# First FFN of a macaron block on one core: norm factors and gates by ScalarE's logarithm and exponential instead of GpSimd's power

## The chip, the cores and the metric

One core of one Trainium2 chip. The metric is device time in microseconds of one execution; several executions are timed and the median is given. The profile is of one execution more, with its own time.

## The reference, cut to what matters

Input x is 8 batch rows of 1024 tokens of 256 numbers, all float32. Three parts follow each other:

```python
x = x + 0.5 * ffn(layernorm(x), ...)
x = x + attn(layernorm(x), ...)
x = x + 0.5 * ffn(layernorm(x), ...)
...
# ffn: 8 experts of 128 hidden units, the best two of each token are used
logits = x @ router_w + router_b
top, idx = top_k(softmax(logits), 2)
top = top / sum(top)                       # the two gates
h = gelu(einsum('btd,nde->btne', x, W1) + b1)
out = sum((einsum('btne,nef->btnf', h, W2) + b2) * mask_with_gates, experts)
# layernorm: (x - mean) / sqrt(var + 1e-5)
```

With l1 and l2 the largest and second largest logit of a token and e = exp(l2 - l1), the two gates are 1/(1+e) and e/(1+e). The kernel puts the factor 0.5 into them, so it computes g1 = 1/(2(1+e)) and g2 = e*g1.

## The kernel before, in words

The core runs five instruction streams (TensorE is PE, VectorE DVE, ScalarE ACT, GpSimd POOL, SyncE SP). Each is written out in program order and meets the others by semaphores.

**First FFN.** Only the two experts that a token chose are computed. The routing runs row by row. A row is 1024 tokens, held as 8 tiles of 128 tokens in one of four buffers `xb` (row r in buffer r % 4). For a row: load (`row_load`, SP); mean and variance (`row_stats`, L1399, DVE, in two halves); the norm's factors rs = (var + eps)^-0.5 and nm = -mean * rs (`row_rstd`, L1899, POOL, with the ALU's power); x * rs + nm in place (`row_norm`, L1123, ACT, in two halves); turn by 128x128 transposes (`row_turn`, L809, PE, copied out by ACT, `row_turned`); logits (`row_logits`, L819, and back to tokens on partitions by `row_logits_turn`, L829); ranks of the logits, the choice and l2 - l1 (`row_route`, L1415, DVE); e = euler ^ (l2 - l1) (`row_exp`, L1913, POOL, power again); both gates into `share` (`row_gates`, L1445, DVE); counting by matmuls of the chosen pattern (`row_spots`, L836, PE) and from it the place of each token in each chosen expert's region (`row_spots`, L1455, DVE). Then `send` (L1917, POOL) issues 16 indirect DMAs per row, one for each tile and choice, which scatter the normed tokens (1 KB each, 128 KB a DMA) to DRAM regions `spots_d`, sorted by expert.

Rows are taken in three batches, rows 0-1, 2-4 and 5-7. When a batch's last row has its spots, `batch_table` (L1478, DVE) makes the table of its blocks: 23, 31 and 31, together 85 **steps** of 256 tokens of one expert. SP then fills each region's end with zeros (`pads`, L587, 8 DMAs of 256 KB) and waits for all sends of the batch (`block_load`, L594). A step is: load a block of 256 tokens (SP); turn it (`block_turn`, PE, L853); copy out (`block_x`, ACT, L1149) with a copy of the expert's W1 (`w1_copy`, ACT, L1164); first matmuls (`block_hidden`, PE, L862); GELU (`block_gelu`, ACT, L1170); second matmuls (`block_out`, PE, L877); add the bias and copy out (`block_left`, DVE, L1538); store to `made_d` (SP).

**What sets the order.** All of it is laid out on hand-written **ticks**. Each engine runs `for tau in range(TICKS)` and in tick tau issues its part of step tau - STEP0 (turn and copy at +0, hidden at +1, GELU at +2, out at +3, bias at +4, store at +5, load at -3) and of every row r whose start `ROW_AT[r]` plus a fixed offset is tau:

| offset | work of a row |
|---|---|
| -5 | load (rows 4 to 7) |
| 0, 1 | statistics, DVE |
| 2 | norm factors, POOL |
| 3, 4 | norm, ACT |
| 4, 5 | turn, PE and ACT |
| 6, 7 | logits, PE and ACT |
| 8 | routing, DVE |
| 9 | count, PE; e, POOL |
| 10 | spots, gates and, at a batch's end, the table, DVE |
| 11 to 16 | sends, three a tick, POOL |
| 12 | at a batch's end, the homes, DVE |

A tick has no clock of its own: an engine goes on as soon as its semaphores allow. Within a tick the order is that of the loop's body (L1039 PE, L1319 ACT, L1773 DVE, L2015 POOL, L635 SP). On SP a tick issues the block store, then the block load, then the row load. The split of the attention's weights in a high and a low part (`split`, six pieces) goes on ACT on the ticks 14, 16 to 24 and on DVE on the ticks 15, 17 to 25.

**After it.** From tick `ROW0` on the first row's results are fetched by indirect DMA (`fetch`, L1925) and added to x with the factors `share` (`combine`, L1541). Then follow 320 attention items over `slots()` and the second FFN, dense over all experts, in 16 groups. The attention's first projections are copied out only after the last step's hidden matmuls (`evac`, L1241), and VectorE goes on only when the last blocks are stored (L1812).

The instruction on which the change turns, L1908:

```python
pool.tensor_tensor(rs_a[:, :], vt_a[:, :], half_a[:, :], ALU.pow).then_inc(s_ars)
```

## Time and profile before

| | us |
|---|---|
| median of 3 executions | 2147.09 (2142.99 to 2148.42) |
| profiled execution, its own time | 2143.95 |
| its span, first to last instruction | 2142.2 |
| TensorE busy | 1899.1 (89%) |
| VectorE busy | 1389.8 (65%) |
| ScalarE busy | 1175.3 (55%) |
| GpSimd busy | 1126.9 (53%) |

The span and the busy times are of the profiled execution. In the rows below an engine's name is followed by the line of the kernel and the operation; `q` behind a name is that engine's queue (register, semaphore and DMA-issuing instructions); "<-" names what ended an idle time, and "remote" or "another core or an unknown queue" is a release that the profile can't place. A busy time doesn't count what the engine waited.

### The profile page before, as it was taken

Reading aid. Unit: us, or ns where it says so; the run is one execution under the profiler, and the core shown is the slowest. Engines: PE = TensorE matmul, PEld = TensorE weight load, DVE = VectorE, ACT = ScalarE, POOL = GpSimd, SP = SyncE. Lnnn points to the kernel's source line nnn. Section 1 sums busy time; section 2 is a strip of 40 time slices with the busy share of each in tenths; the row PEclk is TensorE's granted clock in tenths of the full one; section 3 lists DMA queues with packets and bytes.
Section 4 is the critical chain, followed back from the end, with each engine's and each line's share of the span. In section 5 each row is a group of like instructions: output and inputs, shape, how many; then the busy total and the mean of one; then the engine's idle time right before and its main releaser. Section 6 shows DMA issues by size and latency. Waiting matters only on the chain.

```text
span 2142.2 us, 37969 instructions
## 1 busy us (share of the span) xinstructions
PE 1899.1 (89%) x11764; PEld 1409.7 (66%) x11764; DVE 1389.8 (65%) x4781; ACT 1175.3 (55%) x2936; POOL 1126.9 (53%) x1253
## 2 busy tenths in 40 slices
PE   4377877968998998998998998998999999999998
PEld 2155566845665666665665665665676688888887
DVE  5343344476586585685685685685664488888887
ACT  4244444645557556556556556656555555555554
POOL 5745434157277277377376386386354444444444
PEclk8678988989999999999999999999999999999999
DMA  8557576611031031031031031030023111111110
GB/s 291 194 170 260 197 255 231 233 57 33 1 94 40 1 97 38 1 97 38 1 102 33 1 104 31 3 105 28 1 58 116 37 33 38 40 41 39 36 36 30
DMA packets 106575, 173.64 MB, mean 81 GB/s; under 512 B 13296, under 2 KB 64904, under 8 KB 105480
## 3 DMA queue, kind: packets, MB, share of 16 engines
q1 hardware_dynamic: 83336, 118.42, 16.7%
q0 software_dynamic: 20736, 52.52, 7.8%
q8 instruction: 97, 1.59, 0.3%
q14 instruction: 102, 0.84, 0.1%
q10 hardware_dynamic: 2304, 0.28, 0.1%
HBM read 80.33 MB, written 90.84 MB: 80 GB/s over the span
## 4 chain that ended last, share of the span: by engine, by line
PE 46%; DVE 16%; issue 13%; POOL 12%; ACT 8%; DMA 2%; another core or an unknown queue 1%; SPq 1%; DVEq 0%; ACTq 0%; POOLq 0%
PE bank L720 6%; PE bank L722 5%; PE bank L721 5%; PE bank L1009 4%; PE bank L998 4%; PE bank L969 4%; PE bank L980 4%; PE bank L940 3%; POOL spots_d L1923 3%; ACT prob L1292 2%; POOL prob L1970 2%; DVE x L1550 2%; DVE st L1381 2%; PE bank L971 1%; PE bank L877 1%
## 5 line engine op out<-in xcount | busy, mean ns | idle before, releaser
L1970 POOL TENSOR_TENSOR prob<-prob,rden 128x512 f32<-128x512 f32 x320 | 337.2, 1055 | 452.7 <-DVE rden L1756 449.1
L1292 ACT ACTIVATE prob<-prob,nmax 128x256 f32<-128x256 f32 x512 | 256.0, 502 | 401.8 <-DVE nmax L1738 393.4
L1738 DVE CUSTOM_DVE_ANT_0 prob<-bank,mask 128x256 f32<-128x256 f32 x512 | 195.4, 418 | 105.0 <-PE bank L969 103.5
L1625 DVE SCALAR_TENSOR_TENSOR xb<-bank,gate,xb 128x256 f32<-128x256 f32 x512 | 211.9, 477 | 55.6 <-PE bank L722 55.1
L969 PE MATMUL bank<-kT,qT 64*128 64x256 f32 x1024 | 213.2, 434 | 22.2 <-DVE nmax L1738 21.6
L1885 POOL TENSOR_TENSOR hl<-hf,hh 128x512 fp32r<-128x512 f32 x128 | 164.6, 1291 | 113.9 <-ACT hh L1109 109.2
L980 PE MATMUL bank<-ident,prob 128*128 128x128 f32 x1280 | 199.3, 279 | 20.7 <-POOL prob L1970 20.7
L980 PEld LDWEIGHTS bank<-ident,prob 128*128 128x128 f32 x1280 | 153.9, 142 | 79.9 <-POOL prob L1970 33.3
L1750 DVE COPY probT<-bank 128x512 f32<-128x512 f32 x160 | 110.2, 688 | 117.5 <-PE bank L980 116.6
L1108 ACT ACTIVATE hf<-bank,b1s 128x512 f32<-128x512 f32 x128 | 88.2, 689 | 171.2 <-PE bank L722 167.7
L998 PE MATMUL bank<-probT,V 128*64 128x128 f32 x2048 | 170.7, 288 | 9.1 <-ACT oT_s L1308 7.7
L1538 DVE TENSOR_TENSOR yout<-bank,b_all 128x512 f32<-128x512 f32 x85 | 58.0, 690 | 174.4 <-remote 71.5
L1957 POOL DMA_INDIRECT hs_d<-yr,place x128 | 129.8, 1014 | 44.5 <-issue 32.8
L969 PEld LDWEIGHTS bank<-kT,qT 64*128 64x128 f32 x1024 | 94.9, 188 | 86.5 <-issue 48.2
L998 PEld LDWEIGHTS bank<-probT,V 128*64 128x64 f32 x2048 | 108.8, 137 | 64.4 <-issue 61.0
L1923 POOL DMA_INDIRECT spots_d<-xb,spot x128 | 125.2, 978 | 48.1 <-issue 36.3
L720 PE MATMUL bank<-w,hh 128*128 128x256 f32 x512 | 146.4, 286 | 3.8 <-POOL hl L1885 2.7
L722 PE MATMUL bank<-w,hh 128*128 128x256 f32 x512 | 144.8, 283 | 0.0
L721 PE MATMUL bank<-w,hl 128*128 128x256 f32 x512 | 144.4, 282 | 0.0
L1009 PE MATMUL bank<-wol,oT_s 128*128 128x256 f32 x512 | 126.3, 390 | 1.2 <-ACT xf_t L1239 1.2
L1770 DVE TENSOR_TENSOR x<-bank,x 128x256 f32<-128x256 f32 x64 | 27.1, 423 | 145.3 <-PE bank L1009 145.3
L877 PE MATMUL bank<-w_st,hf 128*128 x340 | 97.0, 411 | 21.3 <-issue 13.6
(254 smaller groups left out, 5016.7 us busy)
## 6 DMA issues: line engine op xcount, KB each, us to landing
xin<-spots_d SPq DMA_DIRECT2D x85, 256.0 KB
made_d<-yout SPq DMA_DIRECT2D x85, 256.0 KB
x<-in_L_attn_x SPq DMA_DIRECT2D x8, 1024.0 KB
x_d<-x SPq DMA_DIRECT2D x8, 1024.0 KB, 4.4
xb<-x_d SPq DMA_DIRECT2D x16, 512.0 KB, 3.8
out<-xb SPq DMA_DIRECT2D x16, 512.0 KB, 2.9
xb<-in_L_attn_x SPq DMA_DIRECT2D x7, 1024.0 KB
spots_d<-zeros SPq DMA_DIRECT2D x24, 256.0 KB
```

The costliest lines, as they stand in the source:

```text
L720: pe.matmul(o, w[0], x[0], start=start, stop=False)
L721: pe.matmul(o, w[1], x[0], start=False, stop=False)
L722: return pe.matmul(o, w[0], x[1], start=False, stop=stop)
L969: ins = pe.matmul(bank[g % NS][:, 0:KEYS], qT[hs, hp, t * P:(t + 1) * P], kT[hs, hp, t * P:t * P + KEYS], start=True, stop=True)
L980: ins = pe.transpose(bank[3 + j % 2][:, (2 * h + kk) * P:(2 * h + kk + 1) * P], prob[j % NP][:, h, kk * P:(kk + 1) * P], ident[:, :])
L998: ins = pe.matmul(bank[5][h * DH:(h + 1) * DH, hp * P:(hp + 1) * P], V[:, t + kk, hs] if t < T else hv[:, kk, hs], probT[j % 2][:, 2 * h + ...
L1009: ins = pe.matmul(bank[tb][:, 0:D], oT_s[:, ch, :], w[:, ch, :], start=(ch == 0), stop=(ch == HC - 1))
L1292: act.activation(prob[j % NP][:, h, :], src, ACT.Exp, bias=nmax[:, j % 4, h:h + 1], scale=-1.0 if light else 1.0, accum_out=den[:, j % 4, ...
L1625: dve.scalar_tensor_tensor(out=x, in0=bank[ob][:, (t % 2) * D:(t % 2 + 1) * D], scalar=gate[:, k % 2, t, e:e + 1], in1=x, op0=ALU.mult, op ...
L1738: ins = dve.tensor_tensor_reduce(prob[j % NP][:, h, :], bank[g % NS][:, 0:KEYS], mask[:, which, :], -1.0, 3e38, ALU.add, ALU.min, nmax[:, ...
L1923: pool.indirect_dma_start(spots_d[batch_of_row(r)], bass.IndirectOffsetOnAxis(spot[:, r, c, t:t + 1], 0), xb[r % 4][:, t, :], None).then_i ...
L1970: pool.tensor_tensor(prob[j % NP][:, :, :], prob[j % NP][:, :, :], rden[:, j % 4, :].unsqueeze(2).broadcast_to([P, 2, KEYS]), ALU.mult).th ...
```

## The change

Row r's norm factors move from GpSimd to ScalarE and VectorE: `row_rstd` on ScalarE takes ln(var + eps) with the eps as a bias from a new tile `eps_a`, then exp(-0.5 * ln), and VectorE's new `row_shift` makes nm in one instruction. Both are issued at offset 2. The exponential for the gates is taken once, for all eight rows, by ScalarE in tick `SHARES` = 62 (`share_exps`), and VectorE makes all gates in tick 63 (`shares`); `t2nd_a` and `wt_a` grow from 128x8 to 128x64 numbers, and `combine` waits for the new semaphore `s_share`. GpSimd keeps only its set-up, the sends, and what it does for the attention. `STEP0` goes from 26 to 24, the rows 3 to 7 start at 18, 26, 35, 44 and 53 instead of 19, 26, 36, 46 and 56, and the split of the attention's weights runs on every tick from 14 (ACT) and 15 (DVE) on. The tile and semaphore declarations and the set-up of `half_a` and `euler_a`, which `eps_a` replaces, are cut here.

```diff
@@ -314,9 +314,10 @@
             return xb_2[k % 3]
 
 
-        STEP0 = 26
+        STEP0 = 24
         TICKS = STEP0 + STEPS + 6
-        ROW_AT = (0, 6, 12, 19, 26, 36, 46, 56)
+        ROW_AT = (0, 6, 12, 18, 26, 35, 44, 53)
+        SHARES = ROW_AT[-1] + 9
 
         def row_at(tau, after):
 
...
@@ -534,7 +535,7 @@
             return 9 + n if n < 5 else 17 + n
 
         NR = 17
-        NA, NPOS, NTAB = 14, 6, 16
+        NA, NPOS, NTAB = 11, 6, 16
         NHOME = 4
         NRK = 1 + 2 * (4 * T - 2) + 2
         TILES = 10 * ROWS
...
@@ -1119,6 +1120,20 @@
                             ffn_hi(kk, n)
                         elif kind == "gt":
                             ffn_gates(kk)
+
+            def row_rstd(r):
+
+                act.wait_ge(s_amv, 2 * r + 2)
+                act.activation(ln_a[:, :], mv_a[:, :, 1], ACT.Ln, bias=eps_a[:, 0:1]).then_inc(s_aln)
+                act.wait_ge(s_aln, r + 1)
+                if r > 0:
+                    act.wait_ge(s_arstd, r)
+                act.activation(rs_a[:, :], ln_a[:, :], ACT.Exp, scale=-0.5).then_inc(s_ars)
+
+            def share_exps():
+
+                act.wait_ge(s_ra, NA * ROWS)
+                act.activation(t2nd_a[:, :, :], t2nd_a[:, :, :], ACT.Exp).then_inc(s_exa)
 
             def row_norm(r, h):
 
...
@@ -1322,9 +1337,13 @@
                 for s_ in step_at(tau):
                     w1_copy(s_)
                     block_x(s_)
+                for r in row_at(tau, 2):
+                    row_rstd(r)
                 for h in range(2):
                     for r in row_at(tau, 3 + h):
                         row_norm(r, h)
+                if tau == SHARES:
+                    share_exps()
                 for what in tick_jobs(tau):
                     evac(*what)
 
...
@@ -1337,8 +1356,8 @@
                     act.wait_ge(s_small, 16 * 8)
                     for at_ in (0, 32):
                         act.activation(b2_s[at_:at_ + E, :], b2_st[:, :], ACT.Copy).then_inc(s_whi)
-                if 14 <= tau < 14 + 2 * 3 * C and tau % 2 == 0:
-                    i, n = (tau - 14) // 2 % C, (tau - 14) // 2 // C * INNER
+                if 14 <= tau < 14 + 3 * C:
+                    i, n = (tau - 14) % C, (tau - 14) // C * INNER
                     split(wqkv_s[0][:, i, n:n + INNER], wqkv_st[:, i, n:n + INNER], (s_wld[4], 16))
 
                 for q in Y0.get(tau, ()):
...
@@ -1407,7 +1426,7 @@
                 ins.then_inc(s_abn)
                 dve.wait_ge(s_abn, 2 * r + h + 1)
                 if h == 0 and r > 0:
-                    dve.wait_ge(s_avar, 2 * r)
+                    dve.wait_ge(s_aln, r)
                 for q in range(TG * h, TG * h + TG):
                     ins = dve.bn_aggr(mv_a[:, q, :], st_a[:, q, :])
                 ins.then_inc(s_amv)
...
@@ -1438,19 +1457,25 @@
                     dve.wait_ge(s_full, job_no["apos", r - 2, 0] + 1)
                 dve.tensor_scalar(chosen[r % 2][:, 0:T, :], lrank[:, :, :], 2.0, None, ALU.is_lt).then_inc(s_ra)
                 dve.wait_ge(s_ra, n + 8)
-                dve.tensor_reduce(t2nd_a[:, :], l2nd[:, :, :], AX_X, ALU.add).then_inc(s_ra)
+                dve.tensor_reduce(t2nd_a[:, r, :], l2nd[:, :, :], AX_X, ALU.add).then_inc(s_ra)
                 dve.wait_ge(s_ra, n + 10)
-                dve.tensor_tensor(t2nd_a[:, :], t2nd_a[:, :], lmax_a[:, :], ALU.subtract).then_inc(s_ra)
-
-            def row_gates(r):
-                n = NA * r
-                dve.wait_ge(s_exa, r + 1)
-                g = share[:, r, :, :]
-                dve.tensor_scalar(wt_a[:, :], t2nd_a[:, :], 1.0, 2.0, ALU.add, ALU.mult).then_inc(s_ra)
-                dve.wait_ge(s_ra, n + 12)
-                dve.reciprocal(g[:, 0, :], wt_a[:, :]).then_inc(s_ra)
-                dve.wait_ge(s_ra, n + 13)
-                dve.tensor_tensor(g[:, 1, :], t2nd_a[:, :], g[:, 0, :], ALU.mult).then_inc(s_ra)
+                dve.tensor_tensor(t2nd_a[:, r, :], t2nd_a[:, r, :], lmax_a[:, :], ALU.subtract).then_inc(s_ra)
+
+            def row_shift(r):
+
+                dve.wait_ge(s_ars, r + 1)
+                if r > 0:
+                    dve.wait_ge(s_anorm, 4 * r)
+                dve.scalar_tensor_tensor(out=nm_a[:, :], in0=mv_a[:, :, 0], scalar=-1.0, in1=rs_a[:, :], op0=ALU.mult, op1=ALU.mult).then_inc(s_arstd)
+
+            def shares():
+
+                dve.wait_ge(s_exa, 1)
+                dve.tensor_scalar(wt_a[:, :, :], t2nd_a[:, :, :], 1.0, 2.0, ALU.add, ALU.mult).then_inc(s_share)
+                dve.wait_ge(s_share, 1)
+                dve.reciprocal(share[:, :, 0, :], wt_a[:, :, :]).then_inc(s_share)
+                dve.wait_ge(s_share, 2)
+                dve.tensor_tensor(share[:, :, 1, :], t2nd_a[:, :, :], share[:, :, 0, :], ALU.mult).then_inc(s_share)
 
             def row_spots(r):
 
...
@@ -1542,6 +1567,7 @@
 
                 if t == 0:
                     dve.wait_ge(s_ald[b % 2], 16 * (b // 2 + 1))
+                    dve.wait_ge(s_share, 3)
                 x = x1[b % 2][:, t, :]
                 for c, part in ((0, y_row), (1, z_row)):
                     dve.wait_ge(s_got[2 * t + c], 16 * (b + 1))
...
@@ -1776,11 +1802,14 @@
                 for h in range(2):
                     for r in row_at(tau, h):
                         row_stats(r, h)
+                for r in row_at(tau, 2):
+                    row_shift(r)
+                if tau == SHARES + 1:
+                    shares()
                 for r in row_at(tau, 10):
                     row_spots(r)
                     if last_of_batch(r):
                         batch_table(batch_of_row(r))
-                    row_gates(r)
                 for r in row_at(tau, 8):
                     row_route(r)
                 for r in row_at(tau, 12):
...
@@ -1794,8 +1823,8 @@
                 if tau == 13:
                     split(rw_s[:, :, 1, :], rw_st[:, :, :], rw_s[:, :, 0, :], 5)
                     split(b2_s[64:64 + E, :], b2_st[:, :], b2_s[0:E, :], 7)
-                if 15 <= tau < 15 + 2 * 3 * C and tau % 2 == 1:
-                    m = (tau - 15) // 2
+                if 15 <= tau < 15 + 3 * C:
+                    m = tau - 15
                     i, n = m % C, m // C * INNER
                     split(wqkv_s[1][:, i, n:n + INNER], wqkv_st[:, i, n:n + INNER], wqkv_s[0][:, i, n:n + INNER], 8 + m)
 
...
@@ -1896,24 +1925,6 @@
                         rstd(0, k + 1, 2 * k + 2)
                     if s == 9 and k < last:
                         exp2nd(k + 1)
-            def row_rstd(r):
-
-                pool.wait_ge(s_amv, 2 * r + 2)
-                if r > 0:
-                    pool.wait_ge(s_anorm, 4 * r)
-                    pool.wait_ge(s_arstd, r)
-                pool.tensor_scalar(vt_a[:, :], mv_a[:, :, 1], LN_EPS, None, ALU.add).then_inc(s_avar)
-                pool.tensor_scalar(nm_a[:, :], mv_a[:, :, 0], -1.0, None, ALU.mult).then_inc(s_avar)
-                pool.wait_ge(s_avar, 2 * r + 1)
-                pool.tensor_tensor(rs_a[:, :], vt_a[:, :], half_a[:, :], ALU.pow).then_inc(s_ars)
-                pool.wait_ge(s_ars, r + 1)
-                pool.wait_ge(s_avar, 2 * r + 2)
-                pool.tensor_tensor(nm_a[:, :], nm_a[:, :], rs_a[:, :], ALU.mult).then_inc(s_arstd)
-
-            def row_exp(r):
-                pool.wait_ge(s_ra, NA * r + 11)
-                pool.tensor_tensor(t2nd_a[:, :], euler_a[:, :], t2nd_a[:, :], ALU.pow).then_inc(s_exa)
-
             def send(r, i):
 
                 t, c = divmod(i, 2)
...
@@ -2013,10 +2023,6 @@
             pool.memset(mask[WIN:P, 2, 3 * WIN:KEYS], MASKED).then_inc(s_const)
             pool.wait_ge(s_const, CONST)
             for tau in range(TICKS):
-                for r in row_at(tau, 2):
-                    row_rstd(r)
-                for r in row_at(tau, 9):
-                    row_exp(r)
                 for i in range(2 * T):
                     for r in row_at(tau, 11 + i // 3):
                         send(r, i)
```

## Rows read from the trace of the kernel before

**Rows 1.** the page: 40 slices of 53.6 us, TensorE's granted clock and DMA share

```profile
PEclk8678988989999999999999999999999999999999
DMA  8557576611031031031031031030023111111110
```

**Rows 2.** the chain that ended last, 84 to 120 us: start, us, what

```profile
91.73 14.96 another core or an unknown queue
```

**Rows 3.** waits, 86 to 420 us: total, times, longest

```profile
DVE yout L1538 <- remote: 71.5, 8, 13.4
...
ACT xa L1136 <- remote: 28.1, 7, 9.3
```

**Rows 4.** block GELUs (L1170) by sending stretch, then overall: length, busy (x)

```profile
86.90:103.80 16.90, 0.00 (x0) 0.80 0.55 181
111.30:131.30 20.00, 0.93 (x2) 0.82 0.69 231
150.20:176.20 26.00, 1.89 (x4) 0.80 0.80 281
196.10:218.70 22.60, 1.42 (x3) 0.85 0.85 286
242.60:265.10 22.50, 2.33 (x5) 0.92 0.69 232
278.30:298.40 20.10, 1.16 (x4) 0.83 0.71 242
...
86.90:416.50 329.60, 41.86 (x86) 0.87 0.66 223
```

**Rows 5.** the sends, groups by line, 0 to 650 us

```profile
L1923 POOL DMA_INDIRECT spots_d<-xb,spot x128 | 125.2, 978 | 48.1 <-issue 36.3 <-DVE spot L1476 11.8
```

**Rows 6.** timeline of GpSimd: start, us, instruction

```profile
35.07 1.23 POOL L1923 DMA_INDIRECT spots_d<-xb,spot  x1 [0.20 <-issue]
...
75.59 0.25 POOL L1905 TENSOR_SCALAR vt_a<-mv_a 128x8 f32<-128x8 f32 x1
...
78.05 1.64 POOL L1915 TENSOR_TENSOR t2nd_a<-euler_a,t2nd_a 128x8 f32<-128x8 f32 x1
...
102.82 0.96 POOL L1923 DMA_INDIRECT spots_d<-xb,spot  x1 [0.31 <-issue]
...
157.27 0.25 POOL L1905 TENSOR_SCALAR vt_a<-mv_a 128x8 f32<-128x8 f32 x1 [3.53 <-DVE mv_a L1412]
```

**Rows 7.** timeline of SyncE's queue, 40 to 92 us: row load, pads, block reads

```profile
61.29 0.40 SPq L585 DMA_DIRECT2D xb<-in_L_attn_x  x1
62.41 15.65 SPq L592 DMA_DIRECT2D spots_d<-zeros  x8
86.88 5.70 SPq L604 DMA_DIRECT2D xin<-spots_d  x3
```

**Rows 8.** ScalarE: timeline, then table loads by line

```profile
42.14 0.20 ACT L1072 ACTIVATE rw<-rw_st 128x16 fp32r<-128x16 f32 x1
...
106.72 0.60 ACT L1149 ACTIVATE xh<-bank 128x512 f32<-128x512 f32 x1 [14.98 <-remote]
107.33 1.28 ACT L1170 ACT_TABLE_LOAD   x1
108.63 0.47 ACT L1170 ACTIVATE hf<-bank,b1s 128x256 f32<-128x256 f32 x1
...
L1292 ACT ACT_TABLE_LOAD x1 | 1.3, 1283 | 0.0
L1108 ACT ACT_TABLE_LOAD x1 | 1.3, 1283 | 0.0
```

**Rows 9.** DMA issues: count, KB each, us to landing

```profile
xb<-in_L_attn_x SPq DMA_DIRECT2D x2, 512.0 KB, 5.2
```

**Rows 10.** timeline of VectorE at 47.5 us

```profile
47.51 0.17 DVE L1443 TENSOR_TENSOR t2nd_a<-t2nd_a,lmax_a 128x8 f32<-128x8 f32 x1
```

**Rows 11.** every engine between two sending stretches: PE, PEld, DVE, ACT, POOL busy

```profile
218.70:242.60 23.90, 20.83 (x103) 15.42 (x104) 10.15 (x32) 11.81 (x27) 1.68 (x2) 0.86 0.51 162
```

More of the change, by code:

```diff
@@ L181, in build @@
         e_row = sb("e_row", [P, len(BATCH), E])
-        half_a, euler_a = sb("half_a", [P, T]), sb("euler_a", [P, T])
+        eps_a = sb("eps_a", [P, 1])
         st_a, mv_a = sb("st_a", [P, T, 6]), sb("mv_a", [P, T, 2])
-        vt_a, rs_a, nm_a = sb("vt_a", [P, T]), sb("rs_a", [P, T]), sb("nm_a", [P, T])
+        ln_a, rs_a, nm_a = sb("ln_a", [P, T]), sb("rs_a", [P, T]), sb("nm_a", [P, T])
         chosen = [sb(f"chosen{i}", [P, T + 1, E], BF16) for i in range(2)]
         lg = sb("lg", [P, T, E])
-        lmax_a, t2nd_a, wt_a = sb("lmax_a", [P, T]), sb("t2nd_a", [P, T]), sb("wt_a", [P, T])
+        lmax_a, t2nd_a, wt_a = sb("lmax_a", [P, T]), sb("t2nd_a", [P, ROWS, T]), sb("wt_a", [P, ROWS, T])
         lrank = sb("lrank", [P, T, E])
@@ L276, in build @@
         s_xa, s_sc = [sem(f"xa_ld{i}") for i in range(4)], [sem(f"sent{i}") for i in range(4)]
-        s_abn, s_amv, s_avar, s_ars, s_arstd, s_anorm = sem("a_bn"), sem("a_mv"), sem("a_var"), sem("a_rs"), sem("a_rstd"), sem("a_normed")
+        s_abn, s_amv, s_aln, s_ars, s_arstd, s_anorm = sem("a_bn"), sem("a_mv"), sem("a_ln"), sem("a_rs"), sem("a_rstd"), sem("a_normed")
         s_ax, s_lq, s_ra, s_exa, s_pos, s_tab, s_zero = sem("xa_turned"), sem("logits_left"), sem("route_a"), sem("exp2_a"), sem("spots"), sem("table"), sem("pads")
-        s_home, s_b2all, s_xa0 = sem("homes"), sem("b2_all"), sem("xa_ld_first")
+        s_home, s_b2all, s_xa0, s_share = sem("homes"), sem("b2_all"), sem("xa_ld_first"), sem("shares")
         s_bld, s_bst = [sem(f"block_ld{i}") for i in range(4)], [sem(f"block_st{i}") for i in range(4)]
@@ L1982, in pool_program @@
             pool.memset(mask[:], 0.0).then_inc(s_const)
-            pool.memset(half_a[:], -0.5)
-            pool.memset(euler_a[:], float(np.e))
+            pool.memset(eps_a[:], LN_EPS)
             pool.iota(token_i[:, :], pattern=[[P, T]], base=0, channel_multiplier=1).then_inc(s_const)
```

## The prediction, made before the changed kernel was run

> **What bounds it now.** I read the page's slices first. From the ninth slice on (after 428 us) the DMA engines are mostly at three tenths or less, and from the tenth on TensorE's granted clock stays at nine tenths or more; ahead of that both swing [rows 1]. The change lies in that stretch, the first FFN, so the question is what sets its length. The chain of waits answers at one place with 15 us in which nothing on the core is busy for the chain [rows 2]. The waits say who stands there: VectorE's copy-out of a block waits 71.5 us in 8 pieces, ScalarE's turned rows 28.1 us in 7, for a release that the trace can't place [rows 3]. Windows then say when. I counted block GELUs, one per step, inside the stretches in which GpSimd sends the rows 2 to 7: 0+2+4+3+5+4 = 18 in 128.1 us. The whole step phase has 85 (and one table load) in 329.6 us, so 67 fall in the other 201.5 us [rows 4]. A step costs 7.1 us while GpSimd sends and 3.0 us while it doesn't. The reader is to see that the bound is neither TensorE nor ScalarE but sending: one send is 0.978 us and 0.30 us of issue, 1.27 us, so 16 of them are 20.4 us a row [rows 5]. Whatever lengthens a sending stretch, or starts it late, is paid.
>
> **GpSimd's share.** It loses per row four instructions, 2.46 us from the first to what follows them, and the power for the gates, 1.64 us [rows 6]. (a) Start. The sends of rows 0 and 1 have to land before the first block is read: they begin at 35.07 and that read is issued at 86.88 [rows 6, 7]. VectorE's tick 8 now holds row 1's shift ahead of row 0's routing, and the shift waits for ScalarE's two loads and two small instructions, 3.0 us [rows 8]; part of that runs while row 0's logits are made. I take half, 1.5 (bounds 0 and 3), so row 0's sends begin at 36.6. From there 32 sends at 1.27 us end at 77.3, and row 2's 16 at 97.7. Now row 2's end at 103.8, the edge of the first window. That is **-6.1 us**. The pads don't stand in the way: they take 15.7 us from 62.4 now, behind the load of row 4 at 61.3 [rows 7], and can begin at about 61 when that load goes behind them. The load of row 4 moves too: it now goes in front of the second block's read. Half a megabyte lands in 5.2 us [rows 9], so 1 MB holds that read 5 to 10 us; I price this at nothing because its cover is the first window, in which no step is done anyway [rows 4]. If that cover is gone, the start's gain goes with it. (b) Shorter windows. Row 4's is 26.0 us, with 3.53 us of waiting for row 5's statistics inside; rows 5 and 6 have 22.6 and 22.5 [rows 4, 6]. At 20.4 each they shrink by 5.6+2.2+2.1 = 9.9 us. A shorter window also does fewer steps: 1 us of it is 0.14 step, worth 0.42 us outside, so 0.58 of it is kept: **-5.7 us**. Bounds: nothing kept (0) and all of it (-9.9).
>
> **ScalarE's share.** Each row gets a logarithm and an exponential of 128x8; the nearest row, 128x16, is 0.20 us [rows 8]. The price is tables. One load is 1.28 us. It starts at 107.33 as the copy before it ends at 107.32, and the GELU starts at 108.63, so nothing but the load is lost [rows 8]. By the Trainium skill (ScalarE: Activation LUTs, What ACT_TABLE_LOAD costs) a switch also drains for about 1.38 us, 2.66 in all, which speaks against this change; this trace shows no such idle time at its GELU load. How many loads a row needs isn't shown, as no logarithm runs: one or two for the pair. I take two, because every kind of function that the trace has after another (GELU, exponential, GELU) was loaded anew [rows 8], and one more brings the GELU back from row 4 on: 3x1.28+2x0.20 = 4.2, with VectorE's shift of 0.17 [rows 10] and three hand-overs of about 0.1 us a row costs 4.7 us of ScalarE's order. (c) Row 4's falls between two windows. There ScalarE is busy 11.8 of 23.9 us beside TensorE's 20.8 [rows 11]; half of 4.7 is hidden, 2.35 is paid. The rows 5 to 7 get their factors one tick after the spots of the row before, as its sends begin. In the windows a microsecond is worth 0.42 and ScalarE is mostly idle: 0.7 each, 2.1. The one exponential for all gates comes outside, with two loads, 2.8 us, half paid: 1.4. Together **+5.85 us**; bounds 0 (all hidden) and 3 x 4.7 + 4.7 + 2.8 = 21.6 (all on the path). What waits behind ScalarE's wait for the last row's routing is that tick's copies; one tick of buffers covers about 2 us of it. The first four rows' loads end before the first block is read and only move row 1, counted in (a).
>
> **VectorE, queues, ticks.** Three small gate instructions leave each row (some 0.5 us) and come back once for 64 columns; the first FFN's combine waits for them much later. I take -0.5. The split of the weights on every tick instead of every second ends before the first block and costs nothing: its cover is GpSimd's sending. Two ticks fewer are no work fewer; rows 9 ticks apart put one row's work into nine steps instead of ten, but the sum of instructions is the same. Taken as 0. After the first FFN nothing changes, and its end passes on in full, because the attention's first projections wait for its last step.
>
> **Sum:** -6.1-5.7+5.85-0.5 = -6.45 us. The profiled execution took 2143.95 us (span 2142.2), 3.1 under the median 2147.09; so 2137.5 for it and **2140.6** as median. A measurement of this kernel can tell about 0.3% from no change, 6.4 us; the forecast lies on that edge.
>
> **Rivals.** *The forecast*, 0.42, from 2132 to 2144, of it 0.30 beyond 0.3% and 0.12 within.
> *The release goes with the sends*: (b) is kept whole and ScalarE's part hides in idle time: -6.1-9.9-0.5 = -16.5, 2130.6. For it: ScalarE waits in every stretch. Against it: it holds block copies in its order. 0.16.
> *The windows are paced by DMA*: in rows 4 and 5 the engines are busy 0.80 and 0.85 at over 280 GB/s [rows 4]; then a window without pauses of GpSimd carries the same bytes and nothing of (b) is kept: -0.75, 2146.3. Against it: rows 6 and 7 have the same 16 sends at 0.69 and 0.71. 0.16 (0.14 within, 0.02 slower).
> *Held hand-overs on ScalarE*, the other side: the factors of rows 5 to 7 need ScalarE, VectorE and ScalarE again just as sends begin, where releases come up to 15 us late [rows 2]; before, GpSimd made them and only the norm waited. Now GELUs and copies of blocks stand behind that wait. The windows of rows 4, 5 and 6 hold 4+3+5 = 12 steps; each lost is 3.0 us, 36 in all. At half of them +18-6.5 = +11.5, 2158.6. It decides from 36% of the 12 steps on. 0.18.
> *A switch with a drain*: each of the step phase's 14 loads would cost as much again as it does here, and a switch would be worth two loads; charged like the loads above (5.85 of 21.6) about +5, 2145.6; all on the path about +18, 2158.6. Rows 8 speak against it. 0.04, half of it slower. By the Trainium skill (ScalarE: Activation LUTs, What ACT_TABLE_LOAD costs), 14 drains of 1.38 are an estimated 19 us.
> *The start doesn't come*: row 4's load or the pads eat (a): 2146.7. 0.04.
>
> Faster 0.30+0.16 = 0.46; within 0.12+0.14+0.02+0.04 = 0.32; slower 0.18+0.02+0.02 = 0.22. The range goes from a little under the second case to a little over the fourth, 2126 to 2160, which takes in the bounds of (b) and most of those of (c).
>
> **What the changed profile would show.** First block read at about 80 us; row 2's sends ending at 98; the windows of rows 4 to 6 at 20 to 21 us, 16 sends each without a pause; 23 table loads of 1.28 us ahead of the attention (two for each of eight rows, one GELU, one more after each of rows 4 to 7, two at the gates), none followed by 1.4 us of idle; GpSimd's waits for VectorE's routing gone; the last block's copy-out 6 us before 416.5. Wrong would be: ScalarE or VectorE waiting some 10 us at the logarithm, the shift or the norm in a window (the fourth case); windows still at 22 to 26 us; a first read at 87; or a step price outside the windows well over 3.0 us, which would put the loads on the path.

## The result: slower by 1.0% where it was timed

The changed kernel takes **2169.11 us** (median of 4, 2168.0 to 2170.64) beside 2147.76 us of the kernel before (median of 4, 2142.99 to 2151.36): a ratio of **1.0101 [1.0080, 1.0123]**. The profiled execution has a span of 2168.1 us at a mean granted clock of 0.956, against 2142.2 us at 0.959. The forecast was 2140.6 us in a range of 2126 to 2160: wrong in sign, and outside the range. All times and intervals here are of executions in the faster of a program's two states.

The page's slices, beside [rows 1]: the clock is a tenth lower in the fifth and sixth slice (217 to 325 us) and has the same digits everywhere else. DMA is lower in the third, fourth and sixth slice and higher in the seventh to the ninth, which end at 488 us.

```profile
PEclk8678878989999999999999999999999999999999
DMA  8546557721022022021031031031013101111110
```

The block GELUs (L1185 now) by sending stretch of row 2 to row 7, then from the first block's read to the end of the last block's copy-out, beside [rows 4]. A stretch in which GpSimd sends one row is called a window here. Columns: stretch, length, ScalarE's busy time on this line (instructions), granted clock, DMA share, GB/s. The counts take in one table load in the windows of rows 2, 4, 5 and 6 and six in the last row. In those of rows 3 and 7 the third instruction is a GELU that began up to 0.3 us before the window and is cut by its edge.

```profile
93.60:113.70 20.10, 1.76 (x2) 0.84 0.35 125
123.80:143.80 20.00, 1.15 (x3) 0.80 0.71 243
165.40:185.70 20.30, 2.23 (x3) 0.86 0.80 273
212.20:232.10 19.90, 2.22 (x3) 0.81 0.87 299
258.60:278.60 20.00, 2.68 (x4) 0.84 0.57 191
299.30:319.40 20.10, 1.11 (x3) 0.93 0.86 310
85.10:440.30 355.20, 48.42 (x91) 0.85 0.64 211
```

Counted by the GELUs that begin in them, the six windows hold 1+2+2+2+3+2 = **12 steps**. The 18 of [rows 4] take in one that began at 277.94, before the last window, so by the same count they were **17**, and all five that are lost are lost in the windows of rows 4 to 6 (4+3+5 before, 2+2+3 now). These three did shrink to 20 us each, from 71.1 us to 60.2; all six from 128.1 to 120.4, since row 2's is no longer cut short by the first read. The other 73 steps take 355.2-120.4 = 234.8 us, 3.22 each, where before 68 took 201.5, 2.96 each. The account closes: -7.7 for the windows, 5 x 2.96 = +14.8 for the steps that they lost, 73 x 0.25 = +18.5 for the price outside, -1.8 for the first read, together +23.8, and 440.3 is 23.8 later than 416.5. It is book-keeping and names no cause yet. The spans differ by 25.9, so the first FFN passes its end on, and 2.1 us more come behind it.

When in a window the steps pass says more. Of the 12 GELUs, 11 begin in the first 9 us of their window and one (273.47) in the remaining 11 us.

The waits of the same phase (engine, tile and line, what it waited for: total, times, longest), beside [rows 3]:

```profile
POOL spots_d L1934 <- DVE spot L1501: 120.1, 6, 26.5
DVE yout L1563 <- remote: 80.5, 10, 17.8
ACT xa L1151 <- remote: 39.0, 5, 12.9
ACT hf L1185 <- remote: 22.2, 3, 10.8
```

GpSimd waits 120 us for spots, where before it waited 58.8 us for VectorE's routing and 11.8 us for spots. VectorE's copy-outs and ScalarE's turned rows wait longer for a release that the trace can't place; one group, ScalarE's block copies, waits less (19.9 us against 24.5). Such waits also stand in the chain that ended last (start, length in us), beside [rows 2]:

```profile
102.94 11.37 another core or an unknown queue
...
132.50 13.42 another core or an unknown queue
...
177.60 10.55 another core or an unknown queue
```

They end at 114.31, 145.92 and 188.15, which is 0.6, 2.1 and 2.5 us after the sends of rows 2, 3 and 4 end (113.7, 143.8, 185.7). Others end while a row is still being sent (VectorE's of 7.6 us at 223.7, in row 5's window). What is held is TensorE's hand-over to ScalarE or VectorE. In the kernel before, the transposes of the second block end at 91.48:

```profile
90.82 0.66 PE L853 MATMUL bank<-ident,xin 128*128 128x128 f32 x4
```

ScalarE's copy of them, which waits for nothing else, starts at 106.72 [rows 8]. That is behind fifteen of row 2's sends and inside GpSimd's work for the next row's factors (103.9 to 107.2); the sixteenth send follows at 109.1. The trace notes the change of that semaphore at 106.69, 0.03 us before ScalarE starts, so it is the increment that comes late and not ScalarE that is slow to see it. In the other direction TensorE follows ScalarE by 0.14 us. Such holds stand beside GpSimd's gathers too, after the last row: it fetches results by unbroken indirect DMA from 350.0 to 367.3 us, and ScalarE's GELU at 368.47 has waited 9.7 us for "remote".

The table loads, on the other hand, are as forecast. Timeline of ScalarE at row 5's factors:

```profile
162.79 0.58 ACT L1164 ACTIVATE xh<-bank 128x512 f32<-128x512 f32 x1
163.39 1.28 ACT L1127 ACT_TABLE_LOAD   x1
164.69 0.30 ACT L1127 ACTIVATE ln_a<-mv_a,eps_a 128x8 f32<-128x8 f32 x1
165.00 1.28 ACT L1131 ACT_TABLE_LOAD   x1
166.30 0.21 ACT L1131 ACTIVATE rs_a<-ln_a 128x8 f32<-128x8 f32 x1
166.53 1.28 ACT L1185 ACT_TABLE_LOAD   x1
167.82 0.47 ACT L1185 ACTIVATE hf<-bank,b1s 128x256 f32<-128x256 f32 x1
```

A load starts as the instruction before it ends and the next function 0.01 to 0.02 us behind it; there are 23 ahead of the attention, two for each logarithm and exponential pair.

The start went otherwise. Row 2's turned rows and logits on ScalarE (number in brackets: idle time before, and its releaser):

```profile
54.31 0.60 ACT L1151 ACTIVATE xa<-bank 128x512 f32<-128x512 f32 x1 [2.93 <-remote]
57.17 0.60 ACT L1151 ACTIVATE xa<-bank 128x512 f32<-128x512 f32 x1 [2.26 <-PE bank L817]
62.12 0.60 ACT L1151 ACTIVATE xa<-bank 128x512 f32<-128x512 f32 x1 [3.83 <-remote]
70.65 0.60 ACT L1151 ACTIVATE xa<-bank 128x512 f32<-128x512 f32 x1 [7.94 <-remote]
81.16 0.59 ACT L1158 ACTIVATE lgT<-bank 8x512 f32<-8x512 f32 x1 [9.39 <-remote]
```

Row 0's sends begin at 36.5, as forecast (36.6), and row 1's end at 78.9; between the two GpSimd does nothing but send. In that stretch row 2's copies are held one by one, 24 us in the four waits for "remote" (2.93+3.83+7.94+9.39). Its spots are there at 93.3 and its sends run from 93.6 to 113.7, not from 77 to 98. In the kernel before the same copies, ready at the same time, went through. GpSimd (L1915) and ScalarE (L1136):

```profile
53.14 1.68 POOL L1915 TENSOR_TENSOR t2nd_a<-euler_a,t2nd_a 128x8 f32<-128x8 f32 x1
...
53.34 1.05 ACT L1136 ACTIVATE xa<-bank 128x512 f32<-128x512 f32 x2
55.18 0.60 ACT L1136 ACTIVATE xa<-bank 128x512 f32<-128x512 f32 x1 [0.27 <-PE bank L816]
56.04 0.60 ACT L1136 ACTIVATE xa<-bank 128x512 f32<-128x512 f32 x1 [0.26 <-PE bank L816]
```

The first two copies begin as ScalarE has finished the norm, so they don't tell when their releases came. But GpSimd had paused twice shortly before, at 46.8 for the factors and at 53.14 for the power of the gates, both of which the change takes off it, and the copies at 55.18 and 56.04 and the logits up to 61.3 get through beside sends that go on without a break from 55.0. In the changed kernel GpSimd has by then sent since 36.5 without one. So here, as in the windows, hand-overs are prompt for the first 6 to 12 us behind a pause and mostly late from then on. That is no fixed figure: in the kernel before, VectorE's copy-out at 123.62 had waited since 114.6, some 5 us behind a pause.

The pads are stretched too, from 15.65 us [rows 7] to 25.73, and the first read stands behind them:

```profile
57.13 25.73 SPq L593 DMA_DIRECT2D spots_d<-zeros  x8
85.14 0.37 SPq L605 DMA_DIRECT2D xin<-spots_d  x1
```

The last send of row 1 is issued by 78.9. In the kernel before, the read followed that send by 2.1 us; here it follows the last pad (82.86) by 2.3. So the pads hold the first read for some 4 us. That is not a wait for TensorE: of SyncE's own eight register moves between them the trace has five at 0.69 to 0.71 us, where all eight take 0.03 in the same program on chip 6 (below).

### The profile page after: what moved, and what is told of

Read it like the earlier page. It is cut to its first block, busy times and chain, and to the rows that moved or that the text cites. A ratio compares the mean times of both kernels' runs of the same rounds, so it can differ in the third digit from the quotient of the medians.

```text
span 2168.1 us, 37951 instructions
## 1 busy us (share of the span) xinstructions
PE 1898.9 (88%) x11764; PEld 1411.9 (65%) x11764; DVE 1388.9 (64%) x4768; ACT 1206.0 (56%) x2974; POOL 1096.9 (51%) x1212
## 4 chain that ended last, share of the span: by engine, by line
PE 49%; DVE 16%; issue 11%; ACT 9%; POOL 8%; another core or an unknown queue 3%; DMA 2%; SPq 1%; DVEq 0%; ACTq 0%; POOLq 0%
PE bank L721 6%; PE bank L723 5%; PE bank L722 5%; PE bank L1010 4%; PE bank L999 4%; PE bank L970 4%; PE bank L981 4%; PE bank L941 3%; PE bank L878 2%; ACT prob L1307 2%; PE bank L863 2%; POOL prob L1981 2%; DVE x L1576 1%; DVE st L1400 1%
## 5 line engine op out<-in xcount | busy, mean ns | idle before, releaser
L1914 POOL TENSOR_TENSOR hl<-hf,hh 128x512 fp32r<-128x512 f32 x128 | 164.8, 1293 | 113.6 <-ACT hh L1110 109.1
L981 PEld LDWEIGHTS bank<-ident,prob 128*128 128x128 f32 x1280 | 153.6, 142 | 81.2 <-POOL prob L1981 34.5
L1776 DVE COPY probT<-bank 128x512 f32<-128x512 f32 x160 | 110.2, 689 | 118.1 <-PE bank L981 117.2
L1563 DVE TENSOR_TENSOR yout<-bank,b_all 128x512 f32<-128x512 f32 x85 | 58.5, 691 | 190.0 <-PE bank L878 81.2
```

The source lines that it names most:

```text
L981: ins = pe.transpose(bank[3 + j % 2][:, (2 * h + kk) * P:(2 * h + kk + 1) * P], prob[j % NP][:, h, kk * P:(kk + 1) * P], ident[:, :])
L1914: pool.tensor_tensor(lo[:, :], f[:, :], h[:, :].bitcast(F32), ALU.subtract).then_inc(s_hl)
```

## The experiments

Eighteen runs of thirteen kernels were made, in five groups, each group on one chip with the kernel before timed between them. **The chips are of two kinds**: on chips 9 and 4 the kernel before takes 2147 to 2148 us, as in the result; on chips 0 and 6 it takes 2084 to 2086 us. Chip 6 was used twice, the others once each, so that it is the chip that decides, and not the occasion, rests on chip 6 alone. The first kind is called "holding" below, for what its traces show. Ratios hold within a group alone. "Steps" are the GELUs that begin in the six windows of rows 2 to 7, where a window leaves out a last send that comes alone behind a pause; by where its edges are laid a count can differ by one or two. "Last out" is where the last copy-out begins, within 0.2 us. The kernel before has 17 steps by this count in its first profile.

| kernel | chip | median us | ratio [95%] | first read | last out | steps |
|---|---|---|---|---|---|---|
| ticks_only | 9 | 2153.34 | 1.0029 [1.0012, 1.0045] | 87.4 | 426.2 | 16 |
| factors_only | 9 | 2160.61 | 1.0068 [1.0045, 1.0090] | 87.7 | 433.9 | 11 |
| gates_only | 9 | 2149.42 | 1.0010 [0.9994, 1.0025] | 84.9 | 420.7 | 16 |
| no_loads | 9 | 2164.65 | 1.0067 [1.0043, 1.0091] | 82.5 | 434.3 | 9 |
| pauses_back | 0 | 2085.34 | 0.9999 [0.9985, 1.0013] | 87.0 | 354.1 | 33 |
| before_paced | 0 | 2084.54 | 0.9991 [0.9971, 1.0010] | 86.3 | 355.2 | 38 |
| dummy_pair | 0 | 2086.45 | 1.0007 [0.9994, 1.0021] | 86.7 | 357.3 | 32 |
| both_old_ticks | 0 | 2079.21 | 0.9960 [0.9945, 0.9975] | 81.2 | 347.3 | 29 |
| after_again | 6 | 2079.28 | 0.9974 [0.9956, 0.9992] | 81.7 | 348.7 | 30 |
| before_again | 6 | 2084.20 | 0.9997 [0.9979, 1.0015] | 86.7 | 355.0 | 33 |
| both_old_ticks_b | 6 | 2077.95 | 0.9955 [0.9933, 0.9977] | 80.4 | 348.1 | 29 |
| factors_back | 6 | 2079.09 | 0.9971 [0.9958, 0.9985] | 85.2 | 349.8 | 31 |
| both_old_ticks_c | 4 | 2167.77 | 1.0086 [1.0054, 1.0118] | 87.4 | 436.4 | 11 |
| dummy_pair_b | 4 | 2150.76 | 1.0018 [1.0004, 1.0033] | 85.5 | 422.6 | 17 |
| before_paced_b | 4 | 2111.73 | 0.9831 [0.9801, 0.9861] | 87.1 | 389.9 | 35 |
| before_paced_c | 6 | 2082.92 | 0.9996 [0.9978, 1.0013] | 87.4 | 356.4 | 38 |
| both_paced | 6 | 2077.86 | 0.9967 [0.9951, 0.9984] | 81.3 | 349.3 | 39 |
| after_paced | 6 | 2077.23 | 0.9964 [0.9942, 0.9986] | 81.7 | 349.0 | 40 |

**The parts alone, on a holding chip.** Each kernel takes one part of the change:

```
ticks_only:    STEP0 24, ROW_AT 9 apart, weight splits on every tick; factors and gates stay on GpSimd
factors_only:  row_rstd on ScalarE, row_shift on VectorE; old ticks, row_exp and row_gates stay
gates_only:    share_exps() and shares() once; old ticks, row_rstd stays on GpSimd
no_loads (the changed kernel):
-  act.activation(ln_a, mv_a[:, :, 1], ACT.Ln, bias=eps_a)      +  ... ACT.Identity, bias=eps_a)
-  act.activation(rs_a, ln_a, ACT.Exp, scale=-0.5)              +  ... ACT.Identity, scale=1.0)
```

> Only the ticks change (STEP0 24, rows at 0, 6, 12, 18, 26, 35, 44, 53, weight split on every tick); factors and gates stay on GpSimd. Held hand-overs on ScalarE (theory 1) and table loads on the path (theory 2): these need the factors on ScalarE, so this is within 6 us of before, 2142 to 2153. Denser ticks (theory 3: steps and rows put closer, so that more of them fall into sending stretches): +15 to +22, 2163 to 2170.

> Only the norm factors go to ScalarE and VectorE; the gates stay on GpSimd per row, ticks as before. Theories 1 and 2: most of the loss is here, +14 to +22, 2162 to 2170. Theory 3: within 6 us of before.

> Only the gates are taken once for all rows by ScalarE (tick 65) and VectorE; factors stay on GpSimd, ticks as before. All theories: within 5 us of before, rather faster, since GpSimd's sends no longer queue behind an exponential (1.64 us a row): 2140 to 2150.

> The changed kernel, but the logarithm and the exponential of the norm factors are replaced by Identity (so the factor is var + eps instead of its power -0.5, near 1 for these inputs; the output is not the reference's): same instructions, order and hand-overs, 19 table loads fewer (24 us of ScalarE). Theory 1: little comes back, 2162 to 2169. Theory 2: most comes back, 2145 to 2155. Theory 3: about half of ScalarE's 24 us at most is on the path, 2158 to 2168.

The parts add up: 0.29+0.68+0.10 = 1.07% beside the 1.01% of the whole. The factors are the large one; the gates alone can't be told from nothing. Ticks only was expected within 6 us of before and costs 5 to 6: with rows 9 apart GpSimd's factor work falls ahead of a row's sends instead of between them, and the windows of rows 4 to 6 hold 2+2+2 steps where before they hold 4+3+5:

```profile
154.90:175.20 20.30, 0.94 (x2) 0.74 0.83 290
198.90:219.00 20.10, 0.93 (x2) 0.83 0.81 284
243.30:263.40 20.10, 0.95 (x2) 0.92 0.59 202
```

This is the nearest thing to a test of the lost steps. In ticks_only ScalarE's order within a tick is that of the kernel before, the rows stand closer, and the pauses in these windows are gone; in factors_only ScalarE's order is changed and the pauses are gone too; both hold 2+2+2 steps there. So the steps lost in these windows go with the pauses, and moving the factors to ScalarE loses none beyond them there. Why the same loss of steps comes to 0.29% in one and 0.68% in the other is shown only in part: the loads (below) are one piece, and the rest wasn't separated.

At the start, a kernel that keeps a GpSimd instruction there (factors_only and ticks_only the power at 53.0 and 53.5, gates_only the factors at 47 to 50) has row 2's first copies at 54.0 to 54.2; in factors_only they had been held for 3.5 us and came free in the pause. In no_loads, where GpSimd only sends, the later copies and the logits are held for 6.0, 9.3 and 9.4 us. Without 19 of the 23 loads the changed kernel is still 0.67% over. The difference to the whole, 0.34% or 7 us, comes from two groups whose intervals overlap, so it is a rough price of the loads; no_loads also leaves its norm factors near 1, and its values are not the reference's.

**Loads, pauses and spreading, first on the other kind of chip.** The edits:

```
pauses_back (the changed kernel), on GpSimd at a row's tick 3, results unused:
+  pool.tensor_tensor(pzo[:, r, :], pz[:, 0, :], pz[:, 1, :], ALU.pow)
+  pool.tensor_tensor(pzq[:, r, :], pz[:, 0, 0:4], pz[:, 1, 0:4], ALU.pow)
dummy_pair (the kernel before), on ScalarE at a row's tick 2, results unused:
+  act.activation(dzo[:, 0, r, :], dz, ACT.Ln, bias=eps_a)
+  act.activation(dzo[:, 1, r, :], dz, ACT.Exp, scale=-0.5)
before_paced (the kernel before), on GpSimd:
-  for r in row_at(tau, 11 + i // 3):
+  for r in [r for r in range(ROWS) if ROW_AT[r] + 11 + i // (2 if r >= 3 else 3) == tau]:
+      if r >= 3 and i % 2 == 0:
+          pool.wait_ge(s_bx, tau - STEP0)
       send(r, i)
both_old_ticks: factors_only and gates_only together
```

> The changed kernel with two unneeded powers on GpSimd (about 2.7 us, on tiles nobody reads) after the third send of the row before, the place where GpSimd's own factor work broke its sends. Theory A (releases of TensorE arrive when GpSimd pauses; a window without pauses holds fewer steps): the windows of the rows 4 to 6 hold one step more each, 3 x 3.0 - 3 x 2.7 x 0.6, 3 to 6 us faster than the changed kernel, 2163 to 2166. Theory B (only ScalarE's work and hand-overs count): 0 to 5 us slower than the changed kernel, 2169 to 2174.

> The kernel before, rows 3 to 7 send two a tick instead of three, each pair waiting until ScalarE has copied out the turned block of the tick before. Theory A: releases get through between the pairs, the sending no longer halts the steps: the 5 windows' 15 lost steps or so come back in part, 10 to 30 us faster than before, 2118 to 2138. Theory B: within 6 us of before. If a late last send delays a batch: up to 10 slower.

> The kernel before with ScalarE's logarithm and exponential at the row's offset 2 for nothing: no waits, results read by nobody, GpSimd still makes the factors. It prices the table loads and nothing else. Theory 1 (hand-overs and order): within 3 us of before. Theory 2 (loads on the path): +5 to +14, 2153 to 2162.

> Factors and gates on ScalarE, ticks as before. If the three parts add up (+0.29%, +0.68%, +0.10% alone): 1.0078 of before, 2164.8. If the denser ticks do their harm only together with ScalarE's factors: 2160 or less.

This group ran on chip 0. There the kernel before is 64 us faster, its first FFN ends near 355 us instead of 416.5, and factors and gates on ScalarE, which add to +0.8% on chip 9, make **-0.4%**. Spreading and loads do nothing that can be measured. pauses_back is an edit of the changed kernel, so its 0.9999 is to be read beside that kernel's 0.9974 on chip 6 (next group): here, where nothing is held, the last copy-out comes 5.4 us later with the two powers a row (354.1 against 348.7), and the change's gain is gone (the two intervals overlap slightly). So these four say nothing of the loss on a holding chip, except that whatever makes it is absent here.

**The changed kernel itself on such a chip.** factors_back is the changed kernel with the factors again on GpSimd.

> The changed kernel once more, next to the kernel before, both profiled on the chip of this call. Theory A (TensorE's releases come late while GpSimd sends, how late depends on the chip, and the change has fewer steps in those stretches): where the kernel before takes about 2148 us the ratio is 1.010 again, 12 of 85 steps in the windows of rows 2 to 7; where it takes about 2084 us the windows hold over 20 steps and the ratio lies between 0.995 and 1.003. Theory B (the chip plays no part): 1.010 on any chip, about 2105 us where before takes 2084.

> The kernel before, profiled on this call's chip. Ratio 1.000 by all theories. Theory A: where it takes about 2148 us its last block is copied out near 416 us with 18 steps in the windows; where it takes about 2084 us near 355 us with over 30 steps in them. Theory B: near 416 us and 18 steps everywhere, and the 64 us between chips lie after the first FFN.

> Factors and gates on ScalarE with rows 10 ticks apart, the same kernel as before under a new name. Theory A: 0.996 where the kernel before takes about 2084 us, and 1.005 to 1.010 where it takes about 2148 us, since the sums of the parts alone gave 1.0068 and 1.0010 there. Theory B: 0.996 everywhere, and the 1 per cent of the changed kernel comes from the ticks.

> The changed kernel with the factors returned to GpSimd; the ticks 9 apart and the gates once stay. Parts that add: 1.0029 x 1.0010 = 1.004 where the kernel before takes about 2148 us. If the factors alone made the loss: 1.000. If they play no part beside the ticks: 1.010. Where the kernel before takes about 2084 us: 1.000 to 1.004, windows of 25 to 32 steps.

The same program that is 1.0% slower in the result is 0.26% faster on chip 6. Its block GELUs there, in the windows of rows 2 to 7 and over all, columns as above:

```profile
80.10:99.90 19.80, 2.71 (x4) 0.81 0.81 266
102.50:122.70 20.20, 3.04 (x7) 1.00 0.90 304
129.80:150.00 20.20, 3.18 (x5) 0.83 0.78 271
164.30:184.20 19.90, 3.17 (x5) 0.83 0.93 316
198.20:218.00 19.80, 4.14 (x7) 1.00 0.75 256
225.70:245.80 20.10, 3.23 (x8) 0.92 0.99 352
81.70:348.70 267.00, 48.49 (x91) 0.94 0.82 280
```

The windows have the length that they have on the other kind of chip, sends at the same pace, but hold 30 steps instead of 12 (counted as above: a load stands in the windows of rows 2, 4, 5 and 6, a step cut by the edge in those of rows 3 and 7). The waits from 86 us to the end of the phase list no "remote" at all, in neither kernel. Row 2's logits, where the changed kernel was held in the result, go through:

```profile
53.64 1.08 ACT L1151 ACTIVATE xa<-bank 128x512 f32<-128x512 f32 x2
56.29 0.59 ACT L1158 ACTIVATE lgT<-bank 8x512 f32<-8x512 f32 x1 [1.05 <-PE bank L827]
```

The kernel before, profiled on the same chip (L1170):

```profile
131.40:156.40 25.00, 2.80 (x6) 0.86 0.82 280
166.20:188.70 22.50, 1.92 (x5) 0.77 0.86 289
...
86.70:355.00 268.30, 41.87 (x86) 0.93 0.81 275
```

On this chip the eight pads take 8.8 us in the kernel before and 9.5 in the changed one, and the trace notes the increment for the second block's transposes 0.02 us behind their end, where the first profile has it 15.2 us late:

```profile
57.03 9.47 SPq L593 DMA_DIRECT2D spots_d<-zeros  x8
```

Between these two kernels the windows shrink from 129.9 to 120.0 us, the 9.9 of the forecast, the first read comes 5.0 us sooner, and three steps move out of the windows at 2.7 us: -9.9-5.0+8.1 = -6.8, and the last copy-out ends 6.3 us sooner. From the last copy-out to the end of the span the kernel before takes 2080.5-355.0 = 1725.5 us here and 2142.2-416.5 = 1725.7 on the chip of its first profile, so the 62 us between those two executions all lie in the first FFN. What is not shown is why the changed kernel's profiled span (2080.6) keeps nothing of its 6.3 us: half is gone by 490 us and the rest by 1662 us, in stages that the change doesn't touch. The medians do keep 5.4 us.

factors_back can't be told from the changed kernel (0.9971): on this kind of chip the ticks with the gates gain, and so do the factors and gates with the old ticks, and the two gains don't add.

**Back on a holding chip.**

> Factors and gates on ScalarE, rows 10 ticks apart, unchanged from the runs of the same kernel that gave 0.996 twice on chips on which the kernel before takes about 2085 us. Theory A (the chip decides how late TensorE's releases come, and on a chip that holds them long the longer chain of the factors loses steps): where the kernel before takes about 2148 us, 1.005 to 1.010, fewer than 14 steps in the windows of rows 2 to 7 and waits of 10 to 18 us for releases that the trace can't place. Theory B (this kernel is better everywhere, the loss of the changed kernel came with the ticks): 0.994 to 0.998 there too.

> The kernel before with a logarithm and an exponential of 128x8 for nothing on ScalarE in each row: it adds the table loads and no dependence. Theory A: the loads alone cost little, 1.000 to 1.003 where the kernel before takes about 2148 us. Theory C (the loads are what costs there, all on the path): 16 loads and up to 8 of the GELU, 24 x 1.28 = 31 us at most, 1.007 to 1.014.

> The kernel before with rows 3 to 7 sending two rows' tiles per tick instead of three, each pair behind a wait for the step's copy on ScalarE, so that steps lie between the sends. Theory A: if the held releases come free in the gaps between pairs, the windows hold over 25 steps instead of 18 and the time falls, 0.985 to 0.997, where the kernel before takes about 2148 us. If they stay held for as long as any sending goes on, the last row's sends come later and the ratio is 1.00 to 1.01.

The kernel that gave 0.9960 and 0.9955 gives 1.0086 on chip 4, near the 0.68+0.10% of its parts on chip 9, with 11 steps in the windows instead of 29. Its waits from 86 to 440 us:

```profile
DVE yout L1563 <- remote: 73.9, 10, 10.1
...
ACT hf L1185 <- remote: 46.8, 5, 11.5
```

Loads with no dependence behind them cost 0.18% [0.04, 0.33], 4 us for 19 more table loads. They leave the windows at 17 steps and rows 2 to 6 within 1.5 us of where they were; row 7's sends start 4.9 us later. So theory C, which asked for 0.7 to 1.4%, falls, and of the factors' 0.68% (chip 9) some 0.5% is not the loads. What is left is the order on ScalarE and the pauses that GpSimd no longer makes; both_old_ticks_c, which has none, holds row 2's copies for 3.5, 5.3 and 8.5 us at the start, as the changed kernel does. For the steps of rows 4 to 6 ticks_only says that it is the pauses. For the rest of the loss the two were not separated: pauses_back, made for that, ran only on the other kind of chip.

Spreading the sends takes **1.7%** off the kernel before (four executions), the largest effect of this study. Its block GELUs (L1170) in the windows of rows 3, 4 and 5 and over all, then its waits from 86 to 395 us:

```profile
113.50:142.70 29.20, 4.26 (x9) 1.00 0.72 240
142.90:174.00 31.10, 2.80 (x6) 0.84 0.82 287
182.00:211.60 29.60, 3.31 (x7) 0.88 0.88 305
...
87.10:389.90 302.80, 41.94 (x86) 0.91 0.73 243
```

```profile
DVE yout L1538 <- remote: 34.3, 8, 9.6
ACT xh L1149 <- remote: 18.6, 3, 14.1
```

The six windows are 28% longer together (164.0 us, 128.1 before) and hold 35 steps instead of 17, 4.7 us a step instead of 7.5; outside them a step takes 2.8 us instead of 2.96. VectorE's wait for the late release halves [rows 3]. With gaps between the sends more hand-overs get through. The longest waits that are left, 15.6 us for VectorE's logits and the 14.1 above, stand at row 2's sends, which were not spread.

**The spread sends with the change.** The same edit on both_old_ticks and on the changed kernel.

> The kernel before with its sends spread (rows 3 to 7: two a tick, each pair behind the step's copy on ScalarE), the same kernel as in the run that gave 0.983. Where the kernel before takes about 2148 us 0.983 again; where it takes about 2085 us 0.999 again.

> Factors and gates on ScalarE, rows 10 ticks apart, the sends of rows 3 to 7 spread in the same way. Theory A (the loss comes from releases held through unbroken sending): where the kernel before takes about 2148 us the factors lose little once sends are spread, 0.978 to 0.988, within 0.005 of the kernel before with spread sends. Rival D (the longer chain of the factors loses steps with or without breaks): 0.99 to 1.00. Where the kernel before takes about 2085 us: 0.994 to 0.997, since little is held there.

> The changed kernel with the sends of rows 3 to 7 spread in the same way. Theory A: where the kernel before takes about 2148 us, 0.978 to 0.990, against 1.010 without the spreading; over 25 steps in the windows instead of 12. Rival D: 0.995 to 1.005. Where the kernel before takes about 2085 us: 0.995 to 0.999.

The chip was one of the other kind again. There after_paced (0.9964) and both_paced (0.9967) can't be told from their versions without spreading (0.9974, 0.9955). Whether after_paced also mends the loss on a holding chip, where theory A would have it between 0.978 and 0.990, was not measured, so rival D, that the longer chain of the factors loses steps with or without gaps, was not tested where it matters.

## Why the prediction was wrong

**Rows and costs that held.** The windows are 20 us without a pause; row 0's sends begin at 36.5; 23 loads of 1.28 us, none with idle time behind it. With that the rival of a switch with a drain is out: the Trainium skill (ScalarE: Activation LUTs, What ACT_TABLE_LOAD costs) gives some 1.38 us of draining beside the load. The trace doesn't agree: behind none of the 23 loads is there more than 0.02 us. The size of (c), +5.85, fits what the loads cost: 4 us (dummy_pair_b), some 7 us (no_loads, rough).

**(a) The start, -6.1, came at -1.8.** Two steps failed. The first is "from there 32 sends at 1.27 us end at 77.3, and row 2's 16 at 97.7": it took row 2's spots for ready. In the kernel before they were, since row 2's copies got through beside GpSimd's pauses at 46.8 and 53.1, which the change removes. Without them they were held for 24 us, and row 2's sends end at 113.7. The second is "The pads don't stand in the way: they take 15.7 us": they took 25.7 and held the first read for some 4 us, so the rival *The start doesn't come* (0.04), by which the pads eat (a), came true in that part. On chip 6, where nothing is held, the same term measures 5.0. One reading was off as well: "Now row 2's end at 103.8" is the end of its fifteenth send; the sixteenth, behind GpSimd's factor work, ends at 110.2.

**(b) The windows, -5.7, turned into a loss.** The length of rows 4 to 6 fell by 10.9 us, where 9.9 was worked out (10.1 on chip 6). What failed is the price of a window's microsecond, "0.14 step, worth 0.42 us outside". It spread the steps of a window evenly over it, and took a pause for waste. On a holding chip most steps pass in the first 9 us or so behind a pause: 10.9 us less of window went with 5 steps fewer, 0.46 step a microsecond and not 0.14. ticks_only shows it from the one side (rows 4 to 6 without a pause, 6 steps instead of 12) and before_paced_b from the other (more gaps, 35 steps).

**(c) "In the windows ScalarE is mostly idle: 0.7 each".** The loads are priced about right. The price of what left GpSimd in exchange, its pauses, stood nowhere in the sum; factors_only has its six windows at 11 steps. Nor did the sum have a term for the steps outside the windows, whose price rose from 2.96 to 3.22 us (+18.5); the loads are 4 to 7 us of that, and the rest stays open.

**The rivals.** *Held hand-overs on ScalarE* had the right outcome and nearly the right size in the windows: it has half of the 12 steps of rows 4 to 6 lost, and 5 were lost there. It was set at 2158.6 because the gains (a), (b) and the rest of the sum were kept beside it, and because nothing was charged for the steps outside. Its mechanism was not the one found: it has the logarithm, shift and norm wait for a late release. The held ones are TensorE's, and ticks_only loses 6 of the same 12 steps with the factors on GpSimd. That the sign was right is luck in that part. *The release goes with the sends* kept (b) whole, and no run here has that: on chip 6 too three steps leave the windows. *Paced by DMA* is out: on chip 6 the same windows carry 256 to 352 GB/s where they carried 125 to 310.

**The point behind all of them.** The forecast was within 0.2 us of what the first FFN did on chip 6 (-6.3 beside -6.45; the median there is 5.4 us down), by luck: the terms were -5.0 and -9.9+8.1 there, not -6.1, -5.7 and +5.85. It was wrong by 28.5 us where it was asked. The profile shown had the sign in it: releases "up to 15 us late" were read as a property of sending as such, which a shorter sending stretch must reduce. They come late in a stretch of unbroken sending, and the change makes the sending unbroken.

## What to carry to other kernels

When a chain shows long waits for a release that no engine's row explains, find out what they coincide with before pricing a pause as waste: removing a pause in the stretch that holds them can cost more than it frees. GpSimd instructions between sends can be such a pause by accident. In such a kernel, try gaps between bursts of indirect DMAs (two per step, tied to a step's own semaphore) before moving work off the sending engine; that was worth 1.7% on one chip of the one kind and cost nothing on two of the other. And time a change of under 1% on more than one chip: here the sign depended on it, for two kernels.

## What was unexpected of the hardware

Two kinds of chip ran the same program in 2148 and in 2084 us, with the same 128 sends at the same pace. All of the difference lay in the first FFN, in releases from TensorE that came up to 15 us late while GpSimd issued indirect DMAs: 71.5 us in VectorE's copy-outs alone on one kind [rows 3], none listed on the other. SyncE is slowed beside the same sends: the first batch's eight pads take 11.2 to 27.9 us in the nine profiles of the one kind and 8.5 to 9.9 us in the eleven of the other. The granted clock differs too in that phase (0.85 and 0.94 over the changed kernel's step phase), but the clock can't be the cause of a gap in which TensorE has finished 15 us before.

Why some chips hold these releases stays open. The semaphore changes late and the waiting engine follows in 0.03 us, so the delay lies with TensorE or on the way; ScalarE's releases to TensorE, in the same windows, arrived in 0.14 us. Every execution timed here was recorded by the profiler too, and the traces with holds lack some records (the block transposes' semaphore changes 77 times in one and 86 in the other of the two profiles of the kernel before). Whether the holds come without the recording was not measured.
